# Attention with routed experts on one core: transpositions of the next batch spread over both side banks, the output product put between the side jobs, and sums of squares ahead of odd row maxima

## What is computed

```
xn  = layernorm(x)
attention: y = layernorm(xn) * g + b;  q = y @ Wq;  k, v = split(xn @ Wkv)      16 heads of 64
           k, v get 2 learned null keys and values per head in front (258 keys)
           q, k = l2norm(q) * q_scale, l2norm(k) * k_scale
           sim = 8 * q k^T - slope_h * |distance|, causal; softmax; @ v; @ Wout
ffn:       shared = (silu(xn @ sg^T) * (xn @ su^T)) @ sd^T
           routed = sum over the top 2 of 8 experts of weight * expert(xn)
```

## Time and profile before

| | |
|---|---|
| median of 3 runs | 492.96 us (492.75 to 495.38) |
| the profiled execution's own time | 497.05 us |
| its span | 495.3 us |
| mean granted TensorE clock | 0.956 of full speed |
| instructions | 10749 |
| PE, DVE, ACT, POOL busy | 427.6, 372.1, 357.9, 322.0 us |
| the batch loop, first scores of batch 0 to the end | from 154.7 us to 495.3 us |
| from one middle batch's scores at step 4 (289.63) to the next one's (332.57) | 42.9 us |

### The profile page before, as it was taken

How to read it: one execution, slowest core, us unless ns; L and a number is a source line. 1 busy time by engine, 2 the same in 40 slices (tenths; PEclk the granted TensorE clock), 3 DMA queues, 4 the chain that set the end, 5 groups by cost and what they waited for, 6 DMA issues and landing times.

```text
span 495.3 us, 10749 instructions
## 1 busy us (share of the span) xinstructions
PE 427.6 (86%) x2809; PEld 307.0 (62%) x2809; DVE 372.1 (75%) x1419; ACT 357.9 (72%) x1098; POOL 322.0 (65%) x492
## 2 busy tenths in 40 slices
PE   4846715999997998999999999999899999989985
PEld 3735413777775766767676666667566666767663
DVE  5698412656653996898799789889888988988884
ACT  3354512666666977988897897899789789878864
POOL 3748779700003789698877968877796897787150
PEclk9959765999999999999999999999999999999999
DMA  8961111222220000000001000000100000010010
GB/s 240 319 217 38 52 50 48 66 80 77 81 66 21 2 13 11 3 23 21 3 1 40 6 1 24 21 3 2 44 1 1 23 23 2 1 43 2 2 44 11
DMA packets 29739, 21.37 MB, mean 43 GB/s; under 512 B 3528, under 2 KB 27376, under 8 KB 29552
## 3 DMA queue, kind: packets, MB, share of 16 engines
q1 hardware_dynamic: 26816, 16.46, 11.2%
q0 software_dynamic: 2048, 4.20, 2.8%
q10 hardware_dynamic: 816, 0.03, 0.1%
HBM read 12.41 MB, written 8.26 MB: 42 GB/s over the span
## 4 chain that ended last, share of the span: by engine, by line
PE 34%; DVE 22%; POOL 18%; issue 11%; ACT 8%; another core or an unknown queue 4%; ACTq 1%; DMA 1%; DVEq 0%; POOLq 0%
PE bank L970 5%; POOL rnorm L425 5%; POOL arena_b L505 4%; DVE arena_b L899 4%; PE bank L972 4%; PE bank L1189 4%; PE bank L971 4%; PE bank L1119 4%; DVE arena_b L914 3%; DVE arena_b L876 3%; PE bank L1110 3%; POOL arena_b L441 2%; POOL rpow L428 2%; DVE probT L924 2%
## 5 line engine op out<-in xcount | busy, mean ns | idle before, releaser
L675 ACT ACTIVATE arena_b<-arena_b,nmx 128x130 f32<-128x130 f32 (+1 forms) x256 | 115.0, 458 | 30.6 <-DVE nmx L899 19.9
L899 DVE CUSTOM_DVE_ANT_0 arena_b<-bank,bias 128x130 f32<-128x130 f32 (+1 forms) x256 | 81.2, 355 | 24.0 <-PE bank L1119 19.0
L914 DVE TENSOR_SCALAR arena_b<-arena_b,rden 128x130 f32<-128x130 f32 (+1 forms) x256 | 82.6, 370 | 4.5
L428 POOL TENSOR_TENSOR rpow<-ssm,mhalf 128x8 f32<-128x8 f32 x32 | 53.0, 1655 | 34.1 <-DVE ssm L887 33.4
L1110 PE MATMUL bank<-ident,arena_b 128*128 128x128 f32 x384 | 67.0, 283 | 5.7 <-DVE arena_b L914 5.6
L441 POOL TENSOR_TENSOR arena_b<-arena_b,rnorm 128x512 f32<-128x512 f32 x64 | 68.1, 1065 | 5.0
L1119 PE MATMUL bank<-arena_a 64*128 64x130 f32 (+1 forms) x512 | 59.5, 351 | 0.8 <-ACT arena_a L636 0.8
L1110 PEld LDWEIGHTS bank<-ident,arena_b 128*128 128x128 f32 x384 | 43.8, 141 | 24.8 <-DVE arena_b L914 13.6
L883 DVE TENSOR_REDUCE ssq<-arena_b 128x8 f32<-128x512 f32 x64 | 43.6, 682 | 14.0 <-issue 13.3
L613 ACT ACTIVATE arena_b<-bank 128x512 f32<-128x512 f32 x64 | 38.1, 596 | 20.8 <-PE bank L972 9.7
L425 POOL TENSOR_TENSOR rnorm<-ssm,mhalf 128x8 f32<-128x8 f32 x32 | 52.8, 1650 | 0.0
(11 more groups left out here) (209 smaller groups left out, 1036.8 us busy)
## 6 DMA issues: line engine op xcount, KB each, us to landing
slot_x<-probT SPq DMA_DIRECT2D x3, 832.0 KB, 8.5
arena_b<-slot_x SPq DMA_DIRECT2D x39, 64.0 KB, 2.0
slot_y<-arena_b SPq DMA_DIRECT2D x39, 64.0 KB, 1.5
arena_a<-in_L_attn_x_dram SPq DMA_DIRECT2D x2, 512.0 KB, 5.2
arena_b<-in_L_ffn_wd_dram SPq DMA_DIRECT2D x1, 1024.0 KB, 9.8
arena_b<-in_L_attn_Wkv_dram SPq DMA_DIRECT2D x1, 1024.0 KB, 8.5
arena_b<-in_L_attn_x_dram SPq DMA_DIRECT2D x8, 128.0 KB, 2.3
out_dram<-arena_b SPq DMA_DIRECT2D x8, 128.0 KB, 1.9
```

What stands on the lines that cost most here:

```text
L428: gp.tensor_tensor(rpow[:, j, :], ssm[:, j, :], mhalf[:, 0:HEADS // 2], ALU.pow).then_inc(g.pw, 1)
L675: sc.activation(prob[:, h % 4, c], sim[h % 2][:, c], ACT.Exp, scale=-1.0, bias=nmx[:, h % HEADS, t:t + 1], accum_out=den[:, h % HEADS, t:t ...
L899: ve.tensor_tensor_reduce(out=sim[h % 2][:, c], in0=bank[h % 2][:, c], in1=bias[:, c], scale=-SLOPES[h], scalar=3e38, op0=ALU.add, op1=ALU ...
L914: ve.tensor_scalar(pr, pr, rden[:, h % HEADS, t:t + 1], None, ALU.mult).then_inc(g.pn, 1)
```

## The change

1. The table of side jobs. Of the four transpositions of the next batch that stood on side 1 at steps 10, 11, 12 and 13, the first stays; the second goes to side 0 at step 9, the third to side 0 at step 10, the fourth to step 14. The keys' job of step 13 goes from side 0 to side 1, and the two values' jobs of steps 14 and 15 go to steps 13 and 14.
2. PE: jobs of side 0 come before the product with Wout, jobs of side 1 behind it; the product with the null values goes from the end of step 5 to its beginning; a wait is added before the scores of head 0 for all of side 1's earlier jobs.
3. ACT: at step 6 the copy of the finished output (yT) comes behind the exponentials and not before.
4. DVE: at odd steps the jobs of side 0 come before the row maxima, and the jobs of side 1 behind.

POOL's order stays as it is. `jobs_until` holds the counting that stood in `jobs`.

```diff
-                 (6, "next", "kq", 0, 0, 1), (7, "prev", "yt", 0, 0, 0), (8, "own", "v", 1, 0, 1), (11, "next", "kq", 1, 1, 1),
...
+                 (6, "next", "kq", 0, 0, 1), (7, "prev", "yt", 0, 0, 0), (8, "own", "v", 1, 0, 1), (9, "next", "tr", 0, 1, 1),
+                 (10, "next", "tr", 0, 0, 0), (11, "next", "kq", 1, 1, 1), (12, "next", "kq", 1, 0, 0), (13, "next", "v", 0, 0, 0),
...
+        def jobs_until(part, b, i, s):
+
+            n = count(part, i, s)
+            if part != "ahead":
+                n = n + count("ahead", i)
...
+            return n
...
@@ ACT @@
-                    if s == 6 and "prev" in whose:
-                        act.wait_ge(g.oread, PAIRS * b)
-                        act.wait_ge(g.fin, b)
-                        sc.activation(yT, bank[6][:, 0:SEQ], ACT.Copy).then_inc(g.yev, 1)
                     h = head_at(part, s, 1)
                     if h is not None:
...
+                    if s == 6 and "prev" in whose:
+                        act.wait_ge(g.oread, PAIRS * b)
+                        act.wait_ge(g.fin, b)
+                        sc.activation(yT, bank[6][:, 0:SEQ], ACT.Copy).then_inc(g.yev, 1)
@@ DVE @@
+                    done = behind(part, b, s, 1)
+                    for job in done:
+                        if job[2][4] == 0:
+                            side_out(*job)
                     if s % 2 == 1:
                         row_maxima(part, b, s)
+                    for job in done:
+                        if job[2][4] == 1:
+                            side_out(*job)
                     h = head_at(part, s, 3)
-                    for job in behind(part, b, s, 1):
-                        side_out(*job)
@@ PE @@
                     todo = jobs(part, b, s)
+                    if s == 5 and "prev" in whose:
+                        pe.wait_ge(g.pn_lo, b)
+                        te.matmul(bank[6][:, 0:SEQ], unull[:], pnT[:], start=False, stop=False)
...
                             pe.wait_ge(g.ttr, TB * (HEADS * b + h))
+                        if h == 0 and part != "first":
+                            pe.wait_ge(left[1], jobs_until(part, b, 1, 0))
...
                     for job in todo:
-                        side_job(job, b)
-                    if s == 5 and "prev" in whose:
-                        pe.wait_ge(g.pn_lo, b)
-                        te.matmul(bank[6][:, 0:SEQ], unull[:], pnT[:], start=False, stop=False)
+                        if job[4] == 0:
+                            side_job(job, b)
                     h = head_at(part, s, 6)
...
+                    for job in todo:
+                        if job[4] == 1:
+                            side_job(job, b)
```

More of the change, by code:

```diff
@@ L263, in behind @@
             return [(part, b, job) for job in jobs(part, b, s - lag)] if part else []
+        def jobs_until(part, b, i, s):
+            n = count(part, i, s)
+            if part != "ahead":
+                n = n + count("ahead", i)
+                if part != "ready":
+                    n = n + count("ready", i)
+                    if part != "first":
+                        n = n + count("first", i) - count("mid", i)
+                        if part == "drain":
+                            n = n + count("last", i) - count("mid", i)
+                        n = b * count("mid", i) + n
+            return n
         def jobs(part, b, s):
@@ L271, in jobs @@
                         continue
-                    n = count(part, i, s)
-                    if part != "ahead":
-                        n = n + count("ahead", i)
-                        if part != "ready":
-                            n = n + count("ready", i)
-                            if part != "first":
-                                n = n + count("first", i) - count("mid", i)
-                                if part == "drain":
-                                    n = n + count("last", i) - count("mid", i)
-                                n = b * count("mid", i) + n
-                    found.append((*job[2:], i, n))
+                    found.append((*job[2:], i, jobs_until(part, b, i, s)))
             return found
```

## The result

The changed kernel takes 496.38 us (median of 8 runs, 495.48 to 498.49), the kernel before 492.97 us beside it: ratio 1.0070, 95% interval 1.0050 to 1.0091. That is 3.4 us slower, where 1.8 us faster was forecast, and 0.6 us outside the range. The time is close to that of the second rival, 496.2 us, which had a chance of 0.15.

The account below looks back on a forecast made before the run. No engine owned the kernel; POOL's sequence alone set the pace for 21.5 of 42.9 us per batch. Terms -0.4 - 0.9 - 0.5 = -1.8 us gave 495.3 from the profiled 497.05, 491.2 against the median 492.96; range 487.0 to 495.8.

Parts of the forecast that it names:

- the second rival: Steps 6 to 8: POOL's operations hold DVE's clamp and an L876, 0.68 us per batch; +3.2 us, 496.2 us, chance 0.15.
- The step that failed: Middle batches, sums taken earlier: DVE and POOL collisions gone and new balance, between -0.44 and about +0.7 per batch, taken as 0.
- the 0.34 us of idle time before head 6's row maxima: DVE, middle batches: idle time expected to absorb part of the 0.62 us delay of a held clamp.
- The point from which the rival was to decide: The second rival decides once DVE's delay at head 6's row maxima exceeds its 0.34 us of idle time.
- Sums ahead of odd row maxima: DVE at step 5: sum of squares starts 0.44 us earlier, and with it POOL's L428, which waits for it.
- the first rival: POOL's lead carries through and DVE's later waits move too: 0.44 + 0.25 us per batch, -5.9 us, 487.1 us, chance 0.40.
- In batch 0, -0.5: Earlier sum starts POOL's unbroken stretch earlier, up to PE's release: -0.5 us at full value, ends 0 and 0.5.
- The product with Wout, -0.9: PE at step 3: the product fills a 0.15 us wait for ACT; 0.15 x 6 = -0.9 us, ends 0 and 1.1.
- The table, 0 in the middle and -0.4 at the end: Step 13 waits mostly go: 0 in six middle batches, covered by POOL's 21.5 us; -0.4 us after batch 6.
- the stall of 0.97 us at step 13: PE's waits of 0.39 us for side 0 and 0.58 us for side 1, which the change was aimed at.
- The new wait, null product and yT, 0: Wait before head 0's scores, null product ahead of step 5, yT copy behind ACT's exponentials: each 0; binding wait's chance 0.04.
- What was to show it: Signs: step 13 waits below 0.4 us, POOL's stretch 21 to 22 us, period 42.7 or 42.8, 43.5 if DVE caught.

Follow-up runs that it names:

- run 12: The changed kernel with DVE's old order at steps 5 and 7, the new one at 3 and 13 alone; ratio 0.9964 to the kernel before.
- run 16: The kernel before, unchanged, for a second profiled execution; ratio 0.9994.
- Run 14: The changed kernel with the clamp written as a max-reduction, DVE's new order kept; ratio 0.9951 to the kernel before, median 490.56 us.
- run 15: The changed kernel with the clamp as a max-reduction and DVE's old order at steps 5 and 7; ratio 0.9975 to the kernel before, median 492.11 us.
- Run 8: The kernel before with only PE's part of the change (product with Wout, null product); ratio 0.9996 to the kernel before.
- run 13: The kernel before with only the new table of jobs and the wait that belongs to it; ratio 1.0003 to the kernel before.
- runs 1: The changed kernel with DVE's old order at all odd steps, row maxima first; ratio 0.9961 to the kernel before.
- run 9: The changed kernel with 26 tiny memsets added on POOL ahead of the norm of step 5, POOL 0.8 us later; ratio 1.0037 to the kernel before.
- runs 14 and 4: The second of these: the changed kernel without the clamp, the sum written where the clamped one was; ratio 0.9918 to the kernel before.

## Why the prediction was wrong, step by step

- **The step that failed**: "Between -0.44 and about +0.7 I take 0: the two collisions that go and the two that come are of the same kind and size." They weren't. Per batch, the first stretch grew by 0.72 us (21.38 to 22.10), or by 0.84 from run 12's 21.26. Batches 1 to 6 all show it, 4.3 us at the first figure. The change gave back 0.2 us in batch 0 and 0.6 us behind the first stretch of batch 6 (61.13 to the end, 61.70 in run 16), which leaves 3.5 us beside the 3.4 us measured. The sizes were not equal: the two collisions that went gave back 0.36 us (L920 at 301.79, 0.55 for 0.91) and 0.31 us (the four L882, 1.74 for 2.05), the two that came took 0.62 and 1.02 us. A row at hand spoke for the loss: in the earlier trace rows the clamp starts at 295.53 and the scaling at 295.54, and POOL was to move forward by 0.44 us.
- **Within that step, a cover that wasn't one**: the 0.34 us of idle time before head 6's row maxima was to hide a part of the clamp's delay. It hid none against run 12: there the row maxima start 13.59 us behind the release with 0.33 us idle before them, in the change 14.07 us, with 0.32 or 0.33 us idle before them still. The point from which the rival was to decide doesn't exist as such.
- **The rival** named the place, the clamp at step 6, correctly. It had the second victim wrong: not an L876 of step 8, but the normalising of head 5 at step 7 (1.57 for 0.55 us), which is the larger of the two. That its price of 0.68 us per batch and the upper end of +0.7 came so near to the measured 0.72 is therefore in good part luck: they leave out a loss of 1.02 us, count one of 0.4 us that didn't come, and take off 0.34 us that hid nothing.
- **Sums ahead of odd row maxima**, as such: right in direction, once nothing is held. Run 14 against run 15 gives -0.22 us per batch in the mean, of the -0.44 of the first rival. In batch 0, -0.5 was forecast: from the first scores to the release, run 14 takes 42.26 us and run 15 42.73, -0.47. In the change itself it was 42.43 beside run 16's 42.63, -0.2.
- **The product with Wout, -0.9**: the right size. Run 8's stretch says -0.11 x 6 = -0.7; the reason was incomplete, since PE gained 0.37 us there and DVE passed on only 0.11.
- **The table, 0 in the middle and -0.4 at the end**: both borne out in the trace of run 13 (21.39 beside 21.38 us; -0.37 us from the release in batch 6 to the end). The reason was wrong: the stall of 0.97 us at step 13 isn't there in run 16. What the table shortens beside run 16 are steps 10 to 12 (4.61 for 4.84 us) and steps 14 to 16 (4.23 for 4.49). In the middle batches PE waits for POOL that much longer at step 1 (1.30 for 0.80 us), as the prediction had said. Nor was the cover complete where the stall did occur: POOL's stretch is 21.54 us in that trace and 21.28 in run 16.
- **The new wait, null product and yT, 0**: in the changed kernel's trace PE is held at step 1 by POOL alone, 1.31 us; runs 1 and 12, which keep all three, are faster than the kernel before.
- **The sum without the failed step and without batch 0**: -0.4 - 0.9 = -1.3 us was forecast, and run 12 shows -1.5 us from the first scores to the end (337.6 for 339.1), -0.36% by its ratio. The error is that of the order on DVE.
- **What was to show it**: less than 4.16 us idle before POOL's first power (3.69), POOL's stretch at 21 to 22 us (21.28), no waits at step 13 (none, but none in run 16 either), and the period of 43.5 us with a long clamp as the sign that DVE was caught; measured 43.38.

## What to carry to other kernels

Before moving an engine's operation forward in time, look at which operations of the engine that it can hold, or be held by (here DVE and POOL), start within a microsecond of each other; here a lead of 0.01 us that happened to be on the right side was worth more than the 0.44 us to be gained. Where such a meeting is unavoidable, try another form of the operation that is caught, not only another order: a reduction in place of a 0.17 us tensor-scalar turned a loss of 0.7% into a gain of 0.5%. Idle time in front of an operation is slack only if it shrinks when the work before it comes late. And take a second profiled execution before a stall that shows in the first is made the target.

## What the runs showed of the hardware that was not expected

It is the form of the two operations that decides, and it is sharper than I had used it. A tensor-scalar of 128x8 that started under POOL's 128x512 multiply, at least 0.1 us before its end, ended 0.02 to 0.04 us behind it in every trace here, whatever its own 0.17 us: 0.28 us long when it started 0.79 us into the multiply (run 12), 1.02 us long when it started 0.05 us into it (run 9). A reduction at the same place took its own 0.17 or 0.68 us (runs 14 and 4). The Trainium skill (SBUF — State Buffer, "Who interferes with whom") has a reason: a tensor-scalar can enter a mode that uses two ports, a reduction cannot on this chip. The traces agree in the times; the ports themselves they don't show.

The rule of the same section of the Trainium skill, that whichever operation comes first holds the pair of ports, would make POOL's power of 128x8, 1.64 us long, the worst of all. It isn't. Run 16, POOL and DVE:

```profile
294.53 1.63 POOL L425 TENSOR_TENSOR rnorm<-ssm,mhalf 128x8 f32<-128x8 f32 x1
...
295.35 0.55 DVE L914 TENSOR_SCALAR arena_b<-arena_b,rden 128x130 f32<-128x130 f32 x2
```

The normalising lies wholly inside the power and takes its undisturbed 0.55 us. A clamp that started 0.06 us into a power took its own 0.17 us (run 12). Why, no run here shows.
